# The projection of attention and MoE 0's dispatch in one block of a two-layer MetaFormer kernel

## What is computed

```python
# layer 0
x = x + _L0_conv_ref(_ln_c(x), L0_conv_w_qkv, L0_conv_w_proj, L0_conv_temperature)
#   its last step: out = jnp.einsum('oc,bchw->bohw', w_proj, out)
t = _to_tokens(x)
t = t + _L0_ffn_ref(_ln_t(t), L0_ffn_router_w, L0_ffn_w1, L0_ffn_b1, L0_ffn_w2, L0_ffn_b2)
#   _moe: logits = tokens @ router_w.T; the two best of 8 experts for every token,
#   y = gelu(tokens @ w1[e] + b1[e]) @ w2[e] + b2[e], weighted and summed
```

## Time and profile before

| | us |
|---|---|
| median of 3 runs | 2374.78 (2374.61 to 2377.22) |
| the profiled execution, its own time | 2370.15 |
| its span | 2368.4 |
| mean granted TensorE clock over the span | 0.914 |
| attention and what stands ahead of it | 0 to 1301 |
| block `project_attention` | 1302 to 1334.5 |
| block `dispatch` of MoE 0 | 1334.7 to 1448 |
| block `experts` of MoE 0 | 1448 to 1589 |
| layer 1 | 1589 to 2368 |

### The profile page before, as it was taken

How to read it: one execution, slowest core, us unless ns; L and a number is a source line. 1 busy time by engine, 2 the same in 40 slices (tenths; PEclk the granted TensorE clock), 3 DMA queues, 4 the chain that set the end, 5 groups by cost and what they waited for, 6 DMA issues and landing times. The chain is left out here.

```text
span 2368.4 us, 84181 instructions
## 1 busy us (share of the span) xinstructions
PE 1993.9 (84%) x29091; PEld 1535.1 (65%) x29092; DVE 2005.2 (85%) x3574; ACT 1770.3 (75%) x2810; POOL 781.3 (33%) x599
## 2 busy tenths in 40 slices
PE   4749999999999999999998724965897339999995
PEld 2426766666666666666666624862685229999994
DVE  5869999999999999999999763759797738888883
ACT  5669999999999999999998663746687626666662
POOL 5321124133222111222124274540264743333331
PEclk8969999999999999999999757986898569999998
DMA  2013323223223223232233253543124722222225
GB/s 85 1 36 86 84 74 91 77 75 94 72 76 93 72 78 91 73 85 84 74 91 107 60 174 108 152 136 112 39 71 135 223 73 49 48 49 49 45 50 158
DMA packets 296699, 203.17 MB, mean 86 GB/s; under 512 B 153579, under 2 KB 277958, under 8 KB 296358
## 3 DMA queue, kind: packets, MB, share of 16 engines
q1 hardware_dynamic: 276838, 166.33, 25.1%
q0 software_dynamic: 19776, 35.73, 5.7%
HBM read 64.79 MB, written 112.92 MB: 75 GB/s over the span
## 5 line engine op out<-in xcount | busy, mean ns | idle before, releaser
L629 DVE TENSOR_TENSOR plow<-prob 128x1024 f16<-128x1024 f32 (+1 forms) x1024 | 1127.6, 1175 | 1.8 <-ACT prob L536 1.8
L536 ACT ACTIVATE prob<-scores 128x1024 f32<-128x1024 f32 x1024 | 998.9, 1026 | 90.4 <-PE scores L689 61.1
L709 PEld LDWEIGHTS outp<-vs,prob 128*128 128x128 bf16 x7680 | 516.0, 98 | 278.9 <-issue 217.6
L709 PE MATMUL outp<-vs,prob 128*128 (+1 forms) x7680 | 604.4, 194 | 26.0 <-DVE plow L629 13.9
L689 PE MATMUL scores<-qT,kT 128*128 (+1 forms) x2048 | 611.6, 380 | 6.3 <-DMA kT<-shift_rows 1.9
L711 PE MATMUL outp<-vs,plow 128*128 (+1 forms) x7680 | 601.7, 194 | 0.0
L711 PEld LDWEIGHTS outp<-vs,plow 128*128 128x128 f16 x7680 | 503.1, 97 | 59.3 <-issue 0.3
L490 POOL TENSOR_TENSOR osum<-osb 128x128 f32<-128x128 f32 x63 | 231.7, 3678 | 832.3 <-DVE rec L634 832.3
L1615 POOL DMA_INDIRECT token_sums<-m1eyo,m1edest x71 | 133.5, 1881 | 277.5 <-DVE m1eyo L1580 134.3
L1450 PE MATMUL m1eph<-m1exT,m1ew1c 128*128 128x128 f16 x3408 | 203.1, 220 | 0.0
L1450 PEld LDWEIGHTS m1eph<-m1exT,m1ew1c 128*128 128x128 f16 x3408 | 194.2, 98 | 0.5
(11 more groups left out here) (397 smaller groups left out, 3389.5 us busy)
## 6 DMA issues: line engine op xcount, KB each, us to landing
sorted_rows<-zero SPq DMA_DIRECT2D x128, 522.0 KB, 4.6
staged<-qk SPq DMA_DIRECT2D x73, 128.0 KB, 2.4
m0exr<-sorted_rows SPq DMA_DIRECT2D x71, 130.5 KB, 2.3
m1exr<-sorted_rows SPq DMA_DIRECT2D x71, 130.5 KB, 2.4
ls_got<-expert_rows SPq DMA_DIRECT2D x8, 1024.0 KB, 5.5
na_staged<-in_L_ffn_W_dram SPq DMA_DIRECT2D x16, 512.0 KB, 3.2
m1dstg<-in_L_ffn_W_dram SPq DMA_DIRECT2D x16, 512.0 KB, 5.3
tok<-in_x_dram SPq DMA_DIRECT2D x8, 512.0 KB, 9.0
```

What stands on the lines that cost most here:

```text
L536: act.activation(prob[g % PBUF][:, :], scores[g % 2][:, :], ACT.Exp, scale=1.0 / (QK_SCALE * QK_SCALE)).then_inc(prob_ready, 1)
L629: dve.tensor_tensor(l[:, 0:n], p[:, 0:n], high(p)[:, 0:n], ALU.subtract).then_inc(low_ready, 1)
L709: pe.matmul(to, high(prob[g % PBUF])[:, cols], v, start=(g == 0 and i == 0 and j == 0), stop=False, skip_group_check=True)
```

## The change

The block `project_attention` is gone. Its work stands in MoE 0's `dispatch`, which gets a `Projection` (with `x_dram`, the buffers and the weights) as a new argument `proj`; for MoE 1 `proj` is None and nothing differs. A table, `joined_order`, says in which order the engines take tiles: ("p", i) is the projection of tile i, ("a", g) the aggregates of group g, ("b", g) its scales, ("d", t) the dispatch of tile t, ("r", g) the route of group g. Each engine walks the same table.

- PSUM: the projection has two buffers of each kind instead of four (`m0dxp`, `m0dpp`); the logits of all groups lie in one place in the bank of `pt`.
- TensorE's first projection now waits for the gate's halves (`gate_step`).
- The norm is taken in four parts of eight tiles instead of two of 8 and 24.
- The weights' 16 parts have eight buffers instead of three (room in `qk`); SP issues their DMAs behind the last of `x`, and `high` and `low` stand behind the last route. The 16 `add_normed` of tiles 16 to 31 stand behind `high`; those of tiles 0 to 15 beside the last group.

In the diff, the first long piece with `if proj:` is DVE's, the last is TensorE's.

```diff
+def joined_order():
+    order = [("p", i) for i in range(G)] + [("a", 0), ("p", G), ("b", 0), ("p", G + 1)]
+    order += [("d", 0), ("d", 1), ("p", 10), ("d", 2), ("d", 3), ("p", 11), ("d", 4), ("d", 5), ("p", 12), ("d", 6),
+              ("p", 13), ("p", 14), ("d", 7), ("p", 15), ("a", 1), ("p", 16), ("b", 1), ("r", 0)]
+    p = 17
+    for g in range(1, NGR):
+        for t in range(g * G, (g + 1) * G):
+            order.append(("d", t))
+            if p < NT:
+                order.append(("p", p))
+                p += 1
+                if p % G == 0:
+                    order.append(("a", p // G - 1))
+        if g + 1 < NGR:
+            order.append(("b", g + 1))
+        order.append(("r", g))
+    return order
...
+            if proj:
+                pl = [pt[:, E_N:E_N + G * E_N].rearrange("p (t e) -> p t e", e=E_N)] * 2
+                xp = [ps(f"xp{u}", [P, 512]) for u in range(2)]
+                pp = [ps(f"pp{u}", [P, 512]) for u in range(2)]
...
             for i, (src, hi, lo, width) in enumerate(parts):
-                if i >= 3:
-                    sp.wait_ge(w_split, i - 2)
-                sp.dma_start(wide(i), src).then_inc(w_in[i % 3], 16)
+                if i >= NS:
+                    sp.wait_ge(w_split, i - NS + 1)
+                sp.dma_start(wide(i), src).then_inc(w_in[i % NS], 16)
...
+            if proj:
+                split_gate()
+                pending = []
+                for kind, i in joined_order():
+                    if kind == "p":
+                        add_projected(i)
+                    if kind in "pa":
+                        for t in pending:
+                            measure(t)
+                        pending = [i] if kind == "p" else []
+                    if kind == "a":
+                        dve.wait_ge(measured, (i + 1) * G)
+                        aggregate(NORM_PARTS[i])
+                    if kind == "b":
+                        scales(i, NORM_PARTS[i])
+                    if kind == "d":
+                        prepare(i)
+                        if i == G:
+                            first_bias_low()
+                    if kind == "r":
+                        route(i)
+                for i in range(NP):
+                    low(i)
...
+            if proj:
+                pending = []
+                for kind, i in joined_order():
+                    if kind == "p":
+                        project(i)
+                    if kind == "d":
+                        turn(i)
+                    if kind in "pdr":
+                        for t in pending:
+                            mult(t)
+                        pending = [i] if kind == "d" else []
+                    if kind == "r":
+                        rank(i)
```

More of the change, by code:

```diff
@@ L1 @@
 from contextlib import ExitStack
+from dataclasses import dataclass
 import concourse.bass as bass
@@ L814, in _ @@
             dve.wait_ge(low_ready, N)
[L817 to L898, removed]
@@ L1183, in scales @@
                                          op1=ALU.mult).then_inc(scaled, 1)
[L1185 to L1192, removed]
@@ new lines, in measure @@
+            def measure(i):
+                dve.wait_ge(summed, i + 1)
+                dve.bn_stats(stats[:, i, :], tok[:, i, :]).then_inc(measured, 1)
+            if proj:
+                split_gate()
[19 more added lines that the diff above has]
+                for i in range(NP):
+                    low(i)
+            else:
+                for c in NORM_PARTS:
+                    aggregate(c)
+                scales(0, NORM_PARTS[0])
+                split_gate()
+                scales(1, NORM_PARTS[1])
+                for t in range(NT):
+                    prepare(t)
+                    if t == G and narrow:
+                        first_bias_low()
+                    if t == 1 and not narrow:
+                        dve.wait_ge(b_turned, 1)
+                        dve.tensor_copy(b1t[:, :, :], pb[:, 0:E_N * NF].rearrange("p (e n) -> p e n", n=NF)
+                                        ).then_inc(b_taken, 1)
+                    if t in route_after:
+                        route(route_after[t])
+                    for i in parts_after(t - LAG):
+                        low(i)
@@ L1272, in _ @@
                 act.activation(b2t, b2t, ACT.Copy, scale=W_SCALE)
-            if add_norm:
+            if add_norm and not proj:
                 for t in range(NT - G, NT):
@@ L1315, in _, with project @@
             pe.wait_ge(gate_step, 3)
-            turn(0)
-            for t in range(NT):
-                if t + 1 < NT:
-                    turn(t + 1)
-                mult(t)
-                if t + 1 in route_after and t + 1 < NT - 1:
-                    rank(route_after[t + 1])
-            rank(NGR - 1)
+            def project(i):
+                xg, n_g = proj.xg, len(proj.xg)
+                if i % GT == 0 and i // GT >= n_g:
+                    pe.wait_ge(x_in[i // GT % n_g], i // GT // n_g * 16)
+                if i % QT == 0 and i:
+                    pe.wait_ge(al_ready, i // QT)
+                if i >= 2:
+                    pe.wait_ge(summed, i - 1)
+                for k in range(KB):
+                    last = pe.transpose(xp[i % 2][:, k * P:(k + 1) * P],
+                                        xg[i // GT % n_g][:, k, i % GT * P:(i % GT + 1) * P], ident32[:, :])
+                last.then_inc(x_turned, 1)
+                n = 0
+                for k in range(KB):
+                    for aa, ww in ((proj.ah, proj.wh), (proj.al, proj.wh), (proj.ah, proj.wl)):
+                        last = pe.matmul(pp[i % 2][:, 0:D], aa[:, i, k * P:(k + 1) * P], ww[:, k, :],
+                                         start=(n == 0), stop=(n == 5))
+                        n += 1
+                last.then_inc(projected, 1)
+            if proj:
+                pending = []
+                for kind, i in joined_order():
+                    if kind == "p":
+                        project(i)
+                    if kind == "d":
+                        turn(i)
[5 more added lines that the diff above has]
+                        rank(i)
+            else:
+                turn(0)
+                for t in range(NT):
+                    if t + 1 < NT:
+                        turn(t + 1)
+                    mult(t)
+                    if t + 1 in route_after and t + 1 < NT - 1:
+                        rank(route_after[t + 1])
+                rank(NGR - 1)
             pe.wait_ge(step, marks[NGR - 1, "seen"])
```

187 lines of the change are left out of this document (132 added, 55 removed).

## The result

The changed kernel takes 2402.81 us (median of 4 runs, 2400.76 to 2405.13), the kernel before 2374.7 beside it: ratio 1.0117, 95% interval 1.0099 to 1.0134. It is slower by 28 to 32 us. The profiled execution has a span of 2403.4 us (before: 2368.4) and a mean granted clock of 0.904 (0.914).

A forecast was written before the change was run, and what follows sets the result against it. It took POOL's scatter queue (64 x 1.31 us) as the bound, now fed late: the stretch grows by 28.2 us, giving 2398.4 on the profiled execution, 2403 with the median's shift; forecast 2400, range 2379 to 2411.

The forecast's parts named there:

- First slots: Group 0's slots, which start the scatters: out at 1355.3, only 1.4 us before the kernel before's 1356.66.
- The gate's wait: TensorE's first projection stands behind the gate's transfer and halves: 4.6 us, so projection starts at 1306.8 instead of 1302.2.
- the double steps: Group 0, three steps of two turns, one projection and two mults: 5.0 us each, 15.1 together.
- the hand-over: From tile 8's projection to the first turn: DVE's sums, aggregates, root, scales, normalisations and first cast take 6.6 us.
- The step: Groups 1 and 2, turn to turn: TensorE and DVE alternate instead of overlapping, 3.9 us at the lower clock, 2.8 at the higher.
- POOL idle: Scatter queue between groups: two idle stretches of about 15 us each, ending when the next group's slots arrive.
- The tail: Weight splits and remaining work behind slots 3: 21 to 29 us, taken as 29, at no cost beside the scatters.
- part 3: Weights behind the last choice; up to 5.5 us more if the 8.4 after the last scatter is not POOL's alone.
- the scatter's price in the last group: POOL's group 3 scatters, starting at 1448.3 with the last at 1467.8; about 1.3 us each.
- The sum: Projection and dispatch stretch, to the experts' first instruction: 1476.2 instead of 1448.0, +28.2 us.
- Rival B: Clock comes back inside the groups: 2389 us, or 2380 if wholly at 2.4 GHz from the start; chance 0.32.
- Rival C: POOL fed without a gap if group 1's step reaches 1.9 us: 2367 to 2373 us; chance 0.06.

The follow-up runs named there:

- A: The changed kernel again, unedited, on another chip beside the kernel before (2370.49 us): 2402.82 us, ratio 1.0130.
- B: The kernel before again, unedited, for its trace on the same chip as A: 2371.43 us.
- experiment G: Changed kernel plus six unread 256-column matmuls after each projection of groups 1 and 2; on two chips with late increments: 2439.58 us (1.0207) and 2446.51 (1.0139).
- experiment C: Changed kernel with DVE's sum of a projection moved behind preparing the next tile, groups 1 and 2; two chips with late increments: 2430.5 us (1.0160), 2440.83 (1.0113).
- experiment E: Changed kernel with both DVE's later sum and the weight splits back among the tiles of groups 1 to 3: 2375.77 us, ratio 1.0014 to the kernel before.
- experiment H: Changed kernel without interleaving: all 32 tiles projected, then groups dispatched in turn, weights last; two chips with late increments: 2414.41 us (1.0088), 2421.47 (1.0039).
- D: Changed kernel with only the weight splits back among the tiles of groups 1 to 3; two chips with late increments: 2443.22 us (1.0205), 2448.59 (1.0159).
- experiment F: Changed kernel with later sum, weights among tiles, projection not waiting for the gate, and POOL's memset moved earlier: 2367.32 us, ratio 0.9984 to the kernel before.

## Why the prediction was right

It said 2400 (2403 with the shift of the median) and slower; measured 2402.8. The mechanism was right; that the number is so close is partly luck. The stretch grew by 31.3 us in the first pair of traces and by 33.4 in A and B, where the prediction has 28.2, and the profiled executions of the first pair differ by 35.0 us (2405.13 against 2370.15), the medians by only 28.1. Its steps, in the first pair of traces:

- *First slots.* Predicted 53.1 us after the block's start, measured 52.9 (before: 54.5). The gate's wait was 4.5 us (4.6), the first turn at 22.5 (22.0), the double steps 5.05, 4.29 and 5.06 (5.0; in the second, the clock was at 2.4 GHz for a moment). Inside the hand-over there is one surprise of 1.8 us, below.
- *The step.* Predicted 3.9 us at the lower clock, measured 3.89 to 4.08, and the granted clock was 0.50 throughout. The 0.3 for the drain of the last matmul, for which rows 5 show no single record, is 0.32 (1361.23 to 1361.55 above). The 2.8 given for the higher clock was measured as 2.85 in experiment G. Slots came 37.0, 35.9 and 20.0 us apart (36.8, 35.4, 19.6).
- *POOL idle* about 15 us twice (15.9, 15.0).
- *The tail.* Predicted up to 29 us behind slots 3, measured 27.0, and at no cost since the scatters end the block. The runs bear this out: DVE's last instruction stands 4.4 us before the next block here and in A, while in experiments C and G, where it ends later, the next block follows it by 1.4 to 1.9. So some 2.5 to 3 us of cover were left. No punctual run moved the tail alone. And the 8.3 to 8.4 us behind the last scatter are the same in runs where DVE has been done for 20 us (8.3 in experiment E): they are POOL's alone, the open point of part 3.
- *The term that was mis-sized* is the scatter's price in the last group: 1.3 us each. It was 1.47 there (1.43 in A), against 1.27 before and 1.30 in experiment E: 2.5 us over the prediction. A's timeline of POOL:

```profile
1448.20 1.50 POOL L1435 DMA_INDIRECT sorted_rows<-m0drows,m0dslots  x1 [0.30 <-issue]
1450.00 1.50 POOL L1435 DMA_INDIRECT sorted_rows<-m0drows,m0dslots  x1 [0.30 <-issue]
1451.81 1.50 POOL L1435 DMA_INDIRECT sorted_rows<-m0drows,m0dslots  x1 [0.31 <-issue]
1453.62 0.97 POOL L1435 DMA_INDIRECT sorted_rows<-m0drows,m0dslots  x1 [0.30 <-issue]
```

and DVE's beside it, nine splits back to back until 1452.5:

```profile
1446.93 5.54 DVE L1058 SCALAR_TENSOR_TENSOR m0w<-qk,m0w 128x512 f16<-128x512 f32 x9
```

The slow scatters stop when the splits do. The weights' transfers were under way too, but the same trace tells the two apart (stages as above, the DMA share is the last but one number):

```profile
1448.00:1452.00 4.00, 0.00 (x0) 0.00 (x0) 4.00 (x8) 0.63 (x1) 3.19 (x3) 0.50 0.73 216
1453.00:1457.00 4.00, 0.00 (x0) 0.00 (x0) 0.00 (x0) 0.59 (x1) 3.09 (x4) 0.50 0.99 329
```

In the second stretch DVE is idle, the transfers are denser (0.99 against 0.73), and the scatters take 0.97 us again. So the long scatters go with DVE's splits, not with the transfers; why is not shown. The other traces agree: with the splits behind the last route the last group's scatters are 1.38 to 1.47 us apart (C, G, H, A and the changed kernel), with the splits among the tiles 1.29 to 1.30 (D, E, F). The tail thus cost 2 to 3 us by slowing the queue that it hid behind.

- *The sum*: predicted +28.2 for the stretch, measured +31.3 in the first pair: 2.5 more from the scatters and 1.1 from the three groups, 0.5 less from other items. In A and B it is +33.4, since B's projection stage took 31.3 us instead of 32.5, and A's first slots came 1.2 later.

The prediction has small slips in its sums, of 0.2 to 2 us, which don't change the forecast. Group 2's scatters, begun at 1427.8, end at 1448.6, not 1448.3. C's last scatter would be 1.6 to 7.8 us earlier than now, not 1.4 to 7.5. B's groups behind slots 0 at 1355.3 give slots 3 at 1435, not 1433.

Rival B (the clock comes back inside the groups) fell: it did not, but for a moment in the second double step, in group 0. A group starts low, as the prediction has it, but pauses of 1.4 to 1.6 us in every step were enough to keep it there for all of groups 1 and 2; in G, where they are filled, and in E, where they are gone, the clock is at 1.00 again. Rival C's condition, 1.9 us per step, was met only by changing the order: experiment E has 1.9 to 2.0 and POOL idles 1.2 to 1.6 us between groups, which is where C was said to decide. The causal claim, that the two engines' order starves the scatter queue, stands on experiments A and E, on one chip, and on the steps of C and G. How the 27 us split between the later sum and the weights' place stays open; the steps (1.6 or 2.4 without the weights, 3.89 with the weights alone) say that nearly all is the order's.

## What to carry to other kernels

When two stages are interleaved on several engines by one list, ask for each step which engine waits for the other's newest result. A step in which A needs B's last and B needs A's last costs the sum of both, and its pauses (here 1.4 to 1.6 us in each 3.9) can hold TensorE's clock down besides; putting the consumer of the slow result one place later on one engine undoes it. Joining stages pays only what the bounding queue (here 64 scatters of 1.3 us) gains at its start, and loses at once when it is fed later than it empties: count the time between feedings, not the busy shares. Work put behind the last feeding is hidden only if it does not slow the queue itself, as DVE's splits did here.

## What the runs showed of the hardware

**DVE held by POOL.** In the changed kernel, ahead of the first turn:

```profile
1322.93 0.19 DVE L1156 RECIPROCAL m0drstd<-m0dsd 128x8 f32<-128x8 f32 x1
1323.16 1.99 DVE L1158 TENSOR_SCALAR m0drstd<-m0drstd 128x8 f32<-128x8 f32 x1
1323.32 1.80 POOL L1430 MEMSET m0w<- 128x2048 f16 x1
```

An instruction of 0.17 us takes 1.99, until POOL's memset ends; in A it takes 1.99 too. With the memset moved (experiment F) the same instruction takes 0.17, and there the gate's two instructions are held by POOL's subtractions instead, for 2.78 and 3.98 us. The sums out of PSUM and the statistics beside the same POOL instructions took their usual 0.42. The Trainium skill (SBUF — State Buffer, section "Who interferes with whom") has it that DVE and GpSimd share a pair of ports as an exclusive lock for a whole instruction, and that `cast` and `tensor_scalar` can ask for it; the trace agrees, and shows that instructions on 8 and 16 columns are held for as long.

**Late increments.** On two of the chips ACT and DVE waited long after TensorE's records had ended. In the first run of experiment H, group 1, nothing but turns and mults is under way:

```profile
1400.83 0.59 PE L1338 MATMUL m0dpx<-ident,m0drows 128*128 128x128 f16 x4
1407.65 0.37 PE L1347 MATMUL m0dpt<-m0dgates,m0dxt 128*128 128x8 f16 x8 [6.24 <-issue]
```

```profile
1399.94 0.60 ACT L1240 ACTIVATE m0dxt<-m0dpx 128x512 f16<-128x512 f16 x1 [3.21 <-remote]
1407.00 0.60 ACT L1240 ACTIVATE m0dxt<-m0dpx 128x512 f16<-128x512 f16 x1 [6.46 <-remote]
```

TensorE's rows stand first, ACT's below. The copy at 1407.00 takes the turn of 1396.53 to 1397.12, ten microseconds late. The trace's semaphore events show it too: in the first run of experiment C, all increments of TensorE before the first scatter (over 2200) come 0.01 us after the record's end; of 72 between 1360 and 1480 us, 30 come over 0.3 us late, the worst 14.5. In A none of 76 does. It happens on each of the eight traces of those two chips, twice with the same kernel and nearly the same steps, and on none of the punctual ones. What follows the block is longer there as well: 936.0 us in that first run against 920.1 in A. I do not know the cause: whether the matmuls themselves end late or only their increments, and whether the scatters bring it on or only stand at the same place. No trace of the kernel before was taken there.
